# A mixture-of-experts block on one core: second biases as selecting products, base rows early, x turned in full tiles

## The reference

```python
h = _layernorm(x, axis=-1) * (1 + cb) + sb
x = x + gb * _L0_ffn_ref(h, ...)
# _L0_ffn_ref, with T = 1024 tokens, width 256, 8 experts of 1024, TOP_K = 2
top_w, top_idx = jax.lax.top_k(router_probs, TOP_K)
top_w = top_w / jnp.sum(top_w, axis=-1, keepdims=True)
cw = jnp.zeros((T, E)).at[jnp.arange(T)[:, None], top_idx].add(top_w)
for e in range(E):
    hmid = jax.nn.gelu(tokens @ w1[e] + b1[e], approximate=False)
    out_e = hmid @ w2[e] + b2[e]
    combined = combined + cw[:, e:e + 1] * out_e
return combined.reshape(b, s, h) + hidden_states
```

## Time and profile before

| | |
|---|---|
| time, median of 3 runs | 290.25 us (289.51 to 292.1) |
| span of the profiled execution | 290.3 us |
| TensorE (PE) busy | 274.4 us, 95% |
| VectorE (DVE) busy | 198.6 us, 68% |
| ScalarE (ACT) busy | 179.7 us, 62% |
| GpSimd (POOL) busy | 121.5 us, 42% |

### The profile page before, as it was taken

How to read it: one execution, slowest core, us unless ns; L and a number is a source line. 1 busy time by engine, 2 the same in 40 slices (tenths; PEclk the granted TensorE clock), 3 DMA queues, 4 the chain that set the end, 5 groups by cost and what they waited for, 6 DMA issues and landing times.

```text
span 290.3 us, 4525 instructions
## 1 busy us (share of the span) xinstructions
PE 274.4 (95%) x1594; PEld 224.0 (77%) x1594; DVE 198.6 (68%) x465; ACT 179.7 (62%) x297; POOL 121.5 (42%) x99
## 2 busy tenths in 40 slices
PE   7989999999999999999999999999999999999980
PEld 2655555468697888776697888999999999999970
DVE  4489599749739759668777386876776768686520
ACT  4238787774495349926885238958769594949100
POOL 8032300000415014484683406548383838566661
PEclk9979999999999999999997599999999999999997
DMA  6990000000008563244179239639295775717133
GB/s 193 382 302 1 2 1 0 0 2 0 0 2 304 167 186 56 72 128 169 46 235 285 64 121 253 175 85 340 77 291 136 224 207 172 210 21 216 20 42 37
DMA packets 32374, 37.94 MB, mean 131 GB/s; under 512 B 7956, under 2 KB 27980, under 8 KB 32332
## 3 DMA queue, kind: packets, MB, share of 16 engines
q1 hardware_dynamic: 26736, 30.10, 32.7%
q0 software_dynamic: 4928, 7.44, 11.4%
q10 hardware_dynamic: 684, 0.06, 0.2%
HBM read 31.63 MB, written 8.90 MB: 140 GB/s over the span
## 4 chain that ended last, share of the span: by engine, by line
PE 70%; DVE 14%; ACT 5%; issue 4%; DMA 2%; POOL 2%; POOLq 1%; DVEq 0%; ACTq 0%
PE bank L1014 19%; PE bank L1043 15%; PE bank L686 8%; PE bank L611 6%; PE bank L783 5%; PE bank L876 2%; PE bank L995 2%; PE bank L1038 2%; PE bank L1037 2%; DVE u L1554 2%; PE bank L622 2%; PE bank L630 1%; DVE xhat L1457 1%; PE bank L640 1%; DMA x_tok<-in_L_attn_x 1%
## 5 line engine op out<-in xcount | busy, mean ns | idle before, releaser
L2065 POOL DMA_INDIRECT out_x<-y_tok,meta x24 | 49.1, 2047 | 46.7 <-DVE y_tok L1907 28.9
L1043 PE MATMUL bank<-w_hi,own 128*128 128x256 f32 x256 | 51.4, 296 | 0.0
L1043 PEld LDWEIGHTS bank<-w_hi,own 128*128 128x128 f32 x256 | 42.7, 200 | 2.3 <-issue 1.6
L1889 DVE TENSOR_TENSOR own<-own_raw,own 128x256 fp32r<-128x256 f32 x64 | 27.1, 424 | 21.0 <-ACT own L1370 16.5
L1014 PE MATMUL bank<-xe_hi,w_hi 128*128 128x320 f32 x128 | 40.1, 313 | 1.5 <-DVE xe_lo L1860 0.8
L1014 PE MATMUL bank<-xe_lo,w_hi 128*128 128x320 f32 x128 | 39.6, 309 | 0.0
L1014 PE MATMUL bank<-xe_hi,w_lo 128*128 128x320 f32 x128 | 39.5, 309 | 0.0
L1364 ACT ACTIVATE own_raw<-bank,b1c 128x320 f32<-128x320 f32 x64 | 33.9, 530 | 8.1 <-PE bank L1014 7.7
L1043 PE MATMUL bank<-w_lo,own 128*128 128x256 f32 x128 | 37.3, 291 | 0.0
L2055 POOL DMA_INDIRECT gb_rows<-gb_table,meta x24 | 24.4, 1015 | 11.7 <-issue 6.7
L1370 ACT ACTIVATE own<-own_raw 128x320 fp32r<-128x320 f32 x64 | 28.8, 462 | 0.0
(11 more groups left out here) (249 smaller groups left out, 626.0 us busy)
## 6 DMA issues: line engine op xcount, KB each, us to landing
e_raw<-in_L_ffn_w SPq DMA_DIRECT2D x16, 1024.0 KB
x_rows<-in_L_attn_x SPq DMA_DIRECT2D x1, 2560.0 KB
xe_tok<-x_rows SPq DMA_DIRECT2D x7, 256.0 KB
raw_m<-in_L_attn_up_W SPq DMA_DIRECT2D x2, 768.0 KB, 9.9
x_tok<-in_L_attn_x SPq DMA_DIRECT2D x2, 512.0 KB, 5.2
out_x<-x_tok SPq DMA_DIRECT2D x1, 1024.0 KB, 5.2
wmod<-in_L_wmod SPq DMA_DIRECT2D x1, 768.0 KB, 11.9
raw_m<-in_L_attn_down_W SPq DMA_DIRECT2D x1, 768.0 KB, 12.6
```

The source lines that it names most:

```text
L1043: ins = nc.tensor.matmul(bank[b][0:n, 0:D], l, r, start=(c == 0 and t == 0), stop=(c == KE - 1 and t == 2))
L1889: nc.vector.tensor_tensor(own_lo[e % 2][:, f, :], own_raw[:, f % 4, 0:whole], own_hi[e % 2][:, f, 0:whole].bitcast(F32), ALU.subtract)
L2065: nc.gpsimd.indirect_dma_start(out_rows, bass.IndirectOffsetOnAxis(ap=ids[0:n, e, k, E:E + 1], axis=0), y_tok[e % 2][0:n, k, :], None, com ...
```

## The change

The bias b2 goes from the base rows into each expert's second layer. A tile of an expert's second layer gets one more product (`bias`): its weights are one column of `of_expert` repeated, which holds ones in rows e and 32+e, and its other operand is `b2_split`, which holds the high parts of b2 in rows 0 to 7 and the low parts in rows 32 to 39 and zero elsewhere. So it adds b2[e] to every slot. It opens tiles 0 and 1 and stands third in tile 2. GpSimd makes both constants near the start. The transposes of the weights, their copies, the eight products and the waits for them go, except in the branch that runs when an expert overflows its 320 slots (not taken here).

`rest` becomes two steps instead of three. Its calls 0 and 1 move into the routing, calls 2 and 3 stay around expert 0's first `keep_y`. The statistics of x2 are taken bank by bank (`x2_stats`).

`turn` loads and transposes three tiles of 128 slots, the last overlapping the second (slots 192 to 319), so that every transpose has 128 rows. The first layer takes the first half of the contraction of blocks 0 to 3, then the second half, then blocks 4 to 7 as before. On ScalarE the high part of expert 2's first weights moves behind expert 0's low rows; on VectorE the low parts of the weights of experts 1 and 2 change places with the low parts of expert 1's blocks. The gathers of expert 0 use another bank.

```diff
-    order.take(("cwT", 0))
+    order.skip(1)
     first_bank = order.next
 
     def take_at(key, n, drains=1):
         order.take(key, drains=drains, bank=(first_bank + n) % 8)
     take_at(("x0", 0), 3, 0)
-    take_at(("x0", 1), 6, 0)
+    take_at(("x0", 1), 1, 0)
     take_at(("xh2", 1, 0), 0, KD)
-    take_at(("places", 1), 1, 2)
+    take_at(("places", 1), 6, 2)
     take_at(("xh2", 1, 1), 2, KD)
     take_at(("h2t", 1, 0), 7)
     take_at(("h2t", 1, 1), 0)
-    take_at(("cwT", 1), 2)
...
-        b2_row = new("b2_row", [D])
+        b2_split = new("b2_split", [D], F32R)
+        of_expert = new("of_expert", [E], F32R)
...
+                        sp.dma_start(xe_tok[e % 2][:, ST - 1:ST, :], b).then_inc(xe_in[e % 2], 16)
...
-                    for k, n in slot_tiles:
-                        ins = nc.tensor.transpose(bank[4 + dt][:, k * P:k * P + n], xe_tok[s][0:n, k, dt * P:(dt + 1) * P], ident[0:n, 0:n])
+                    for k in range(ST):
+                        at_ = min(k * P, CAP - P)
+                        ins = nc.tensor.transpose(bank[4 + dt][:, at_:at_ + P], xe_tok[s][:, k, dt * P:(dt + 1) * P], ident[:])
                     end(ins, 4 + dt)
 
             def first_layer(e, at_f=None, between=None):
                 s = e % 2
                 pe.wait_ge(w1_hi_done, e + 1)
                 pe.wait_ge(w1_lo_done, e + 1)
-                for f in range(KE):
+
+                def part(f, c):
+                    b, _, need = order.at[("s1", f % 4)]
+                    if c == 0:
+                        pe.wait_ge(drained[b], e * (KE // 4) + need + f // 4)
+                    for t, (l, r) in enumerate(three([w[s][:, c, f * P:(f + 1) * P] for w in (w1_hi, w1_lo)], (xe_hi[s][:, c, :], xe_lo[s][:, c, :]))):
+                        ins = nc.tensor.matmul(bank[b][:, 0:CAP], l, r, start=(c == 0 and t == 0), stop=(c == KD - 1 and t == 2))
+                    if c == KD - 1:
+                        end(ins, b)
+
+                for c in range(KD):
+                    pe.wait_ge(xe_hi_done, e * KD + c + 1)
+                    pe.wait_ge(xe_lo_done, e * KD + c + 1)
+                    for f in range(KE // 2):
+                        part(f, c)
+                for f in range(KE // 2, KE):
                     if f == at_f:
                         between()
-                    if e == 1 and f < TT // 2:
-                        pe.wait_ge(bias_read, f + 1)
-                    b, _, need = order.at[("s1", f % 4)]
-                    pe.wait_ge(drained[b], e * (KE // 4) + need + f // 4)
                     for c in range(KD):
-                        if f == 0:
-                            pe.wait_ge(xe_hi_done, e * KD + c + 1)
-                            pe.wait_ge(xe_lo_done, e * KD + c + 1)
-                        for t, (l, r) in enumerate(three([w[s][:, c, f * P:(f + 1) * P] for w in (w1_hi, w1_lo)], (xe_hi[s][:, c, :], xe_lo[s][:, c, :]))):
-                            ins = nc.tensor.matmul(bank[b][:, 0:CAP], l, r, start=(c == 0 and t == 0), stop=(c == KD - 1 and t == 2))
-                    end(ins, b)
-
-            def bias_of(i):
-                b, _, need = order.at[("s1", i)]
-                pe.wait_ge(drained[b], need + KE // 4)
-                second_bias(i)
+                        part(f, c)
+
+            def bias(e, b, n, start):
+
+                return nc.tensor.matmul(bank[b][0:n, 0:D], of_expert[:, e:e + 1].to_broadcast([P, n]), b2_split[:], start=start, stop=False)
...
+                    if n == P:
+                        bias(e, b, n, True)
                     for c in range(KE):
                         if e == 0 and k == 0:
                             pe.wait_ge(own_lo_done, c + 1)
@@ -1038,14 +1044,11 @@
                             ins = nc.tensor.matmul(bank[b][0:2 * n, 0:D], own[s][:, c, k * P:k * P + 2 * n], w2_hi[s][:, c, :], start=(c == 0), stop=(c == KE - 1))
                             if c == 0:
                                 nc.tensor.matmul(bank[b][0:n, 0:D], own_hi[s][:, c, k * P:k * P + n], w2_lo[s][:, c, :], start=False, stop=False)
+                                bias(e, b, n, False)
                             continue
                         for t, (l, r) in enumerate(three([g[s][:, c, k * P:k * P + n] for g in (own_hi, own_lo)], (w2_hi[s][:, c, :], w2_lo[s][:, c, :]))):
-                            ins = nc.tensor.matmul(bank[b][0:n, 0:D], l, r, start=(c == 0 and t == 0), stop=(c == KE - 1 and t == 2))
-                        if e == 0 and k == 0 and c % 2 and c < KE - 1:
-                            bias_of(c // 2)
+                            ins = nc.tensor.matmul(bank[b][0:n, 0:D], l, r, start=False, stop=(c == KE - 1 and t == 2))
                     end(ins, b)
-                    if e == 0 and k == 0:
-                        bias_of(TT // 2 - 1)
...
-            keep_weights(0)
             ln_root(4)
             norm2(1)
             numerators(1)
             modulate_last()
             keep_h2(1)
-            keep_weights(1)
...
-                w1_hi_of(2)
                 w2_hi_of(1)
                 x_hi(1)
-                act.wait_ge(bias_read, TT // 2)
+                act.wait_ge(rest_done, TT // 2)
                 keep_low(0)
+                w1_hi_of(2)
...
+            def x2_stats(hf):
+
+                tiles = []
+                for p in range(2):
+                    b, ps = full(("x2t", hf, p))
+                    some = [(hf * TH + 2 * p + q, ps[:, q * D:(q + 1) * D]) for q in range(2)]
+                    ready = bn_stats_of(some)
+                    tiles += some
+                aggregate(tiles, ready)
...
-                nc.vector.tensor_tensor(rt[:, 5, ts, :], rt[:, 3, ts, :], across(big[:, ts]), ALU.mult).then_inc(top_done, 1)
...
+            def rest(i):
+
+                hf, k = i // 2, i % 2
+                if i == 0:
+                    dve.wait_ge(gbb_in, 16)
+                until_drained(("h2t", hf, k))
+                until_drained(("x2t", hf, 1), 1 if hf else 2)
+                st.link(nc.vector.tensor_tensor(bits[:], h2_rows[:, 2 * i:2 * i + 2, 0:D], gb_of(i), ALU.mult))
+                nc.vector.tensor_tensor(x2_tok[:, 2 * i:2 * i + 2, :], x2_tok[:, 2 * i:2 * i + 2, :], bits[:], ALU.add).then_inc(rest_done, 1)
+                dve.wait_ge(rest_done, i + 1)
...
             v_of(KF + 5)
+            rest(0)
             dve.wait_ge(v_lo_done, NH * KF - 1)
             dve.wait_ge(v_hi_done, NH * KF)
             nc.vector.tensor_tensor(v_lo[:, KF - 1, hs[1]], v_tile[(NH * KF - 1) % 4], v_hi[:, KF - 1, hs[1]].bitcast(F32), ALU.subtract).then_inc(v_lo_done, 1)
             x2_of(1, [0])
             w1_lo_of(0)
             pick(0)
+            rest(1)
             x2_of(1, [1])
-            ln_stats(x2_tiles(1))
+            x2_stats(1)
...
-                dve.wait_ge(bias_made, i + 1)
-                g = gbb[:, 2 * i * P // S:2 * i * P // S + 1, :].to_broadcast([P, 2, D])
-                st.link(nc.vector.tensor_tensor(bits[:], bank[i][:].rearrange("p (q d) -> p q d", q=2), h2_rows[:, 2 * i:2 * i + 2, 0:D], ALU.add))
-                dve.sem_inc(bias_read, 1)
-                st.link(nc.vector.tensor_tensor(bits[:], bits[:], g, ALU.mult))
-                nc.vector.tensor_tensor(x2_tok[:, 2 * i:2 * i + 2, :], x2_tok[:, 2 * i:2 * i + 2, :], bits[:], ALU.add).then_inc(rest_done, 1)
-                dve.wait_ge(rest_done, i + 1)
...
-                rest(0)
-                rest(1)
+                rest(2)
                 keep_y(0, 0)
-                rest(2)
+                rest(3)
                 keep_y(0, 1)
-                rest(3)
                 x_lo(1)
                 keep_y(0, 2)
-                w1_lo_of(2)
+                w2_lo_of(1)
                 for f in range(KE):
+                    if f == 2:
+                        w1_lo_of(2)
+                    if f == 4:
+                        x_lo(2)
                     own_lo_of(1, f)
-                    if f == EARLY - 1:
-                        x_lo(2)
-                w2_lo_of(1)
...
+            nc.gpsimd.tensor_tensor(of_expert[:], ident[:, 0:E], ident[:, 32:32 + E], ALU.add).then_inc(b2_step, 1)
+            nc.gpsimd.memset(b2_split[:].bitcast(F32), 0.0).then_inc(b2_step, 1)
...
+            for k, at_ in enumerate((0, 32)):
+                pool.wait_ge(b2_step, 2 + k)
+                nc.gpsimd.tensor_scalar(b2_split[at_:at_ + E, :], b2_row[at_:at_ + E, :], 1.0, None, ALU.mult).then_inc(b2_step, 1)
+            pool.wait_ge(b2_step, 4)
+            lo(b2_split[32:32 + E, :], b2_row[32:32 + E, :], b2_split[32:32 + E, :], b2_ready)
```

85 lines of the change are left out of this document (51 added, 34 removed).

## The result

The changed kernel takes 294.5 us (median of four executions, 293.3 to 296.3) against 290.3 for the kernel before in the same session: a ratio of 1.020 (1.015 to 1.025). By either it is slower. The forecast was 284.0 us, with 287.8 as the upper end.

A forecast was written before the change was run, and what follows sets the result against it. TensorE, busy 95% of the span, was taken as the bound, with the gate rows the new bound at expert 0. Terms -7.4 + 2.6 - 3.2 + 1.7 = -6.3 us took 290.3 to 284.0 us, range 281.0 to 287.8.

The forecast's parts named there:

- selecting products: Experts 1 to 7: 21 added products at 0.124 us, +2.6 us, at most +4.6; GpSimd's preparation of their constants: nothing.
- signs of being wrong: Gate rows landing much before 160 or after 163, new TensorE waits in expert 2, or a growing later-expert period.
- Base: Starting time: profiled span 290.3 us, median of three runs 290.25, so no offset was taken.
- The stretch before expert 0: Routing: two early base-row steps cost +0.15 us by 129.9; router's results come 0.3 us earlier net.
- Expert 0: Second layer ends near 156.9, gate rows at 160.7 become the bound, expert 1 starts at 163.7 instead of 171.09: -7.4 us.
- The clock: TensorE's wait at expert 0, 156.9 to 163.7: a half-clock fall is likely, +1.7 us, bounds 0 and 5.1.
- the terms were 2.99 and 1.7: Expert 0: 2.99 us from gate rows at 160.7 to expert 1's start at 163.7; 1.7 us for half clock.
- Expert 2's weights: ScalarE's moved high part and VectorE's order in expert 1 taken as nothing; expert 2 up to 1.9 us later if cover fails.
- The cover that the prediction names: Expert 1's first activation comes 15 products, 2.3 us, after its first layer begins, so ScalarE's 1.90 us step fits.
- turns: Six full-height turns of x in later experts save 0.53 us each: -3.2 us, at least -1.0.
- The rival that ends slower: Expert 0's gate rows: eleven GpSimd transfers slowed beside denser VectorE work, 16 us added, 300 us; chance 0.04.

## Why the prediction was wrong

The step that failed is the last sentence on the selecting products: "GpSimd prepares their constants in a few steps on small tiles near the start; it is busy 42% of the span, and they are first used at 151 us: nothing." The steps are small, but the first waits for b2 until 21.2 us, and `wm_lo`, which nobody had moved, is queued behind it. Held, it runs beside VectorE's convolution and stops it for 6.7 us (11.29 against 4.55), where TensorE had other products for 1.7 us only (28.1 to 29.8 before). Moving the constants behind it gave 6.6 us back; putting the wait into the kernel before cost 4.5. The 2 us between the two are about what two differences of medians can be off, and are not resolved; in the profiled executions the stretch from `xn` to `rbuf` is 6.5 us longer in the changed kernel and 7.9 longer in the kernel before with the wait. I had asked who waits for the constants, and not what is queued behind the instruction that waits for their input. Two of the prediction's own signs of being wrong came: gate rows after 163, and a new wait at expert 2.

Point by point:

- *Base.* The profiled execution was taken to lie at the median. It lay 1.8 us above it, with 1.9 us lost before `xn` of the first half, and its half-clock stretch at expert 0 is in some executions only. The forecast from the same terms is 285.8.
- *The stretch before expert 0.* "I count +0.15 us by 129.9" was too little by more than 1 us. I had filled VectorE's gap of 1.14 us with a base-row step of 1.55 (0.83 + 0.73 are 1.56, and two instructions without a subtraction beside them take 1.45, as from 134.06 to 135.51 after); the first of its two instructions alone takes 1.75 while GpSimd subtracts. By the traces the early rows cost the routing 1.5 us.
- *Expert 0.* Right in kind: no L876, products 0.12 us apart, the gate rows as the new bound, VectorE's order behind it. In the changed kernel they land at 168.5, because all ahead of them is late; with the two losses undone VectorE has them at 159.7, a microsecond ahead of the forecast. Some of that is luck: this profiled execution did not lose the 1.9 us at its start that the one of the forecast had lost.
- *The clock.* The fall behind the wait came as forecast, 6.8 us at half in place of 3.4. It pushes the third tile past VectorE, and with late rows 4.6 us lie between the gate rows and expert 1; the terms were 2.99 and 1.7. With the tile off the gate rows, four of five profiled executions have no half clock there; the fifth, the one with the low parts in pieces, has 3.4 us of it behind its unexplained wait.
- *Expert 2's weights.* "I take as nothing ...": expert 2 lost 1.1 us with the rows late, and in the changed kernel 0.7 (8.95 us behind expert 1; 8.77 before, less the 0.53 of a turn, is 8.24). The cover that the prediction names, for ScalarE's step of 1.90, held. What failed is VectorE's order in expert 1, which the same sentence put at nothing and no cover was given for.
- *Selecting products* 0.117 us each (0.124 taken), *turns* 0.53 us each by the periods: right.
- *The rival that ends slower* named the right pair of engines, in the wrong place. It priced GpSimd's scatters held up by VectorE; what happened was VectorE's convolution held up by GpSimd.

With the constants and the rows moved, 286.75 us are measured where the terms say 285.8. As the traces have them, the constants' place costs 6.5 us, the early rows 1.5 and expert 2's weights 0.7 in the changed kernel: 8.7, which is also what lies between 285.8 and the result. That the sum closes so well is partly luck, for the medians carry about 1 us of doubt each, the base is one execution, and the early rows' part was not told from nothing by the timings. Only the first term was shown both by taking it out and by putting it into the kernel before.

## What to carry over

Of an instruction that is added to a queue, cost the wait first: list what stands behind it on its engine, and look what each of these will run beside when it is late. Before putting work on GpSimd, look which VectorE steps with operands in SBUF are on the chain in that stretch; here an overlap cost such a step nearly the whole length of the subtraction. And read which execution a profile is of, its clock stretches above all, before a difference is taken from it.

## What the runs showed of the hardware

- Some of VectorE's steps on operands in SBUF stand still while GpSimd subtracts 128x1536 (3.43 us): 0.76 became 3.94 us for a step with two such inputs, the four of `xhat` took 3.73 instead of 1.38, and even a 128x2 step of 0.17 us became 0.87. Not all do: beside the same subtraction in the kernel with `wm_lo` held until the convolution is done, a reciprocal of 128x4 in SBUF took 0.18 us as elsewhere (27.88), and `xn`, with one input in SBUF and one in PSUM, 1.41 (30.30). The modulation (L1506, L1528), which reads PSUM, took 1.9 us for four steps beside the subtraction and without it.
- GpSimd waits too. The subtraction that began 0.08 us behind the start of a VectorE step is recorded with 3.95 us, against 3.44 for one that found VectorE between two steps.
- The half clock at a product is not fixed by what TensorE executes there. The eight-row products took about 1.13 us for each of their four groups in the one profiled execution of the same code (kernel before, `wm_lo` held until the convolution is done), and 1.13, 1.13, 2.07 and 2.07 in the profile before.
